# A stack of graph layers in lots: layer 3's first message three lots sooner, and a new plan of who makes which blocks

## The reference, cut to what matters

```python
h = relu(layernorm(x));  x = x + L0(h)      # pairwise attention
h = relu(layernorm(x));  x = x + L1(h)      # edge-gated aggregation
h = relu(layernorm(x));  x = x + L2(h)      # masked attention with tanh and exp
h = relu(layernorm(x));  x = x + L3(h)      # 5 steps of a gated recurrent unit
# L0: for all pairs of nodes i, j of a batch
pre = s1[i] + s2[j] + b                     # 256 features
e[i, j] = sum(a * leaky_relu(pre)) + adj    # then softmax over j, times x, sigmoid
# L3: one step
m = adj @ h;  z, r = gates(m, h);  hv = tanh(... m, r * h);  h = (1 - z) * h + z * hv
```

## Time and profile before

| | us |
|---|---|
| median of 3 runs | 5592.85 |
| lowest and highest | 5590.37, 5593.27 |
| the profiled execution, its own time | 5579.68 |
| its span, first to last instruction | 5577.9 |

### The profile page before, as it was taken

The page is one execution under the profiler, slowest core; times in us unless marked ns, Lnnn a source line. Parts: engine busy times, 40 slices in busy tenths (PEclk is TensorE's granted clock), DMA queues, the critical chain, the costliest instruction groups (busy, mean ns, idle before and its releaser), DMA issues.

```text
span 5577.9 us, 115796 instructions
## 1 busy us (share of the span) xinstructions
PE 5428.9 (97%) x38790; PEld 2133.7 (38%) x38790; DVE 5093.6 (91%) x9843; ACT 5086.3 (91%) x13332; POOL 4831.1 (87%) x9606
## 2 busy tenths in 40 slices
PE   8999999999999999999999999999999999999997
PEld 2333333333333333333333433333333333333334
DVE  8999999999998999999999999999999999999993
ACT  8999999999999999999999999999999999999993
POOL 8988888889888888889888888888898888889880
PEclk9999999999999999999999999999999999999998
DMA  0000000000000000000000000000000000000000
GB/s 14 3 4 7 7 6 3 6 7 7 6 7 3 6 7 7 6 3 6 7 7 6 5 4 7 7 7 6 3 6 7 7 6 3 6 7 7 6 6 6
DMA packets 44233, 33.97 MB, mean 6 GB/s; under 512 B 4736, under 2 KB 39552, under 8 KB 43648
## 3 DMA queue, kind: packets, MB, share of 16 engines
q1 hardware_dynamic: 43648, 26.56, 1.6%
HBM read 9.77 MB, written 8.39 MB: 3 GB/s over the span
## 4 chain that ended last, share of the span: by engine, by line
PE 93%; POOL 2%; DVE 2%; issue 2%; ACT 1%; DMA 0%; SPq 0%; POOLq 0%; DVEq 0%
PE S L1108 58%; PE R L1052 15%; PE S L1052 5%; PE W L1052 4%; PE V L1052 3%; PE R L1250 3%; POOL ring L570 2%; PE R L1258 1%; PE S L1099 1%; ACT ring L902 1%; PE V L1135 1%; DVE ring L699 1%; POOL signed L561 1%; PE R L1147 1%; PE W L1147 0%
## 5 line engine op out<-in xcount | busy, mean ns | idle before, releaser
L902 ACT ACTIVATE ring<-V,U_minus 128x256 f32<-128x256 f32 x10496 | 4114.8, 645 | 5.6 <-issue 5.6
L1108 PE MATMUL S<-ring,a_window 128*32 128x512 f32 x30720 | 3493.8, 598 | 107.9 <-issue 79.6
L570 POOL TENSOR_SCALAR ring<-W,U 128x256 f32<-128x256 f32 x7040 | 3424.6, 501 | 19.6 <-PE S L1108 19.6
L699 DVE TENSOR_TENSOR ring<-U,W 128x1024 f32<-128x1024 f32 (+2 forms) x2592 | 2662.7, 1064 | 7.1 <-ACT V L926 7.1
L1108 PEld LDWEIGHTS S<-ring,a_window 128*32 128x32 f32 x30720 | 914.4, 110 | 2396.8 <-issue 2349.2
L561 POOL TENSOR_SCALAR signed<-W_signed,U_ceiling,U_floor 128x256 f32<-128x256 f32 x2048 | 1166.5, 571 | 105.2 <-DVE ring L690 104.9
L694 DVE TENSOR_TENSOR ring<-U,W 128x256 f32<-128x256 f32 x2176 | 854.5, 409 | 0.1
L690 DVE SCALAR_TENSOR_TENSOR ring<-W,U,signed 128x256 f32<-128x256 f32 x2048 | 825.0, 470 | 2.2 <-POOL signed L561 2.2
L532 POOL TENSOR_TENSOR rstd<-var,minus_half 128x4 f32<-128x4 f32 (+1 forms) x160 | 148.8, 930 | 309.6 <-DVE var L725 171.6
L1052 PE MATMUL R<-mT,W 128*128 128x512 f32 (+1 forms) x640 | 334.0, 604 | 2.7 <-ACT mT L1012 2.7
L1052 PE MATMUL R<-AT,h 128*128 128x256 f32 x1264 | 326.9, 404 | 2.1 <-ACT h L1024 2.1
(11 more groups left out here) (185 smaller groups left out, 4282.7 us busy)
## 6 DMA issues: line engine op xcount, KB each, us to landing
X<-in_x SPq DMA_DIRECT2D x64, 128.0 KB, 2.1
X_held<-X SPq DMA_DIRECT2D x32, 256.0 KB, 2.4
out<-OUT SPq DMA_DIRECT2D x64, 128.0 KB, 1.9
edge<-in_L_gnn_w_w SPq DMA_DIRECT2D x3, 128.0 KB, 2.1
A<-in_adj SPq DMA_DIRECT2D x1, 256.0 KB, 2.7
Wn<-in_L_gnn_Wn SPq DMA_DIRECT2D x1, 128.0 KB, 2.5
Wm<-in_L_gnn_Wm SPq DMA_DIRECT2D x1, 128.0 KB, 2.5
weight<-in_L_gnn_u_w SPq DMA_DIRECT2D x2, 64.0 KB, 2.1
```

Source lines behind the costliest of these rows:

```text
L570: last = gp.tensor_scalar(ring[:, place, g, half * N:(half + 1) * N], W[:, y, c], LARGEST, U[:, y, c, i:i + 1], ALU.min, ALU.max)
L699: piece = dve.tensor_tensor(ring[:, place, g:g + groups].rearrange("p g (h j) -> p g h j", h=NB), u.unsqueeze(3).to_broadcast([P, groups, ...
L902: last = act.activation(ring[:, place, g, half * N:(half + 1) * N], W_scalar[y][:, c * N:(c + 1) * N], ACT.Relu, bias=U_minus[:, y, c, i:i ...
L1108: last = pe.matmul(S[y][g * ROWS:(g + 1) * ROWS, :], a_window[:, c, ROWS - 1 - row:2 * ROWS - 1 - row], ring[:, place, g], start=False, st ...
```

## The change

The transposes of layer 3 and its h3T copy move to lots 115 and 118, and the first message, alone of all steps, to lot 115, so that TensorE does both behind lot 112. The output copy moves from lot 113 to 112. The plan books half of each stage's cost 3 lots ahead of the stage (`AHEAD`), has other numbers for several stages, one more entry for GpSimd (7 at each half's start) and a lower start cost for GpSimd's share.

```diff
-LN3 = dict(stats=107, factors=109, norm=111, transpose=118, copy=120)
-L3_FROM, L3_PERIOD = 118, 25
-L3 = dict(message=0, ..., transpose=21, back=23)
+LN3 = dict(stats=107, factors=109, norm=111, transpose=115, copy=118)
+L3_FROM, L3_PERIOD, L3_FIRST_MESSAGE = 118, 25, 115
+L3 = dict(message=0, ..., transpose=21, out=22, back=23)

-... POOL_BLOCK, POOL_START, VECTOR_SUMMED, POOL_SIGNED = ... 4.5, 1.0, 3.92, 5.33
+... POOL_BLOCK, POOL_START, VECTOR_SUMMED, POOL_SIGNED = ... 4.5, 0.1, 3.92, 5.3
+AHEAD = 3

+    def book(costs, t, cost):
+        costs[t % LOTS] += cost / 2
+        costs[(t - AHEAD) % LOTS] += cost / 2
     def put(costs, table, at, **stages):
         for name, cost in stages.items():
-            costs[at + table[name]] += cost
+            book(costs, at + table[name], cost)

-        put(scalar, POST[h], half, exp=10, copy=4.8, tanh=5)
+        put(scalar, POST[h], half, exp=8, copy=3, tanh=5)
-        put(scalar, PRE[h], half, norm=7.7, copy=3.6, evacuate=30)
+        put(scalar, PRE[h], half, norm=7.7, copy=2.7, evacuate=32)
+        book(pool, half, 7)
-        put(scalar, ln, 0, norm=10, copy=4.8)
+        put(scalar, ln, 0, norm=15.4, copy=4.8)
-        for stage, cost in dict(update=6, state=18).items():
+        for stage, cost in dict(update=7, state=18, out=6 if s == STEPS - 1 else 0).items():

         def layer3_at(turn, t):
-            pair = turn.m - 1 if t >= L3_FROM else turn.m - 2
-            step, p = divmod((t - L3_FROM) % LOTS, L3_PERIOD)
+            pair = turn.m - 1 if t >= L3_FIRST_MESSAGE else turn.m - 2
+            if t == L3_FIRST_MESSAGE:
+                step, p = 0, L3["message"]
+            else:
+                step, p = divmod((t - L3_FROM) % LOTS, L3_PERIOD)
+                if step == 0 and p == L3["message"]:
+                    step = STEPS

-                    if p == L3["back"] and s == STEPS - 1:
+                    if p == L3["out"] and s == STEPS - 1:
```

More of the change, by code:

```diff
@@ L100 @@
 L2 = dict(project=78, copy=81, scores=86, tanh=89, exp=90, mask=93, aggregate=103, residual=106)
-LN3 = dict(stats=107, factors=109, norm=111, transpose=118, copy=120)
-L3_FROM, L3_PERIOD = 118, 25
-L3 = dict(message=0, copy=3, gates=5, reset=9, update=11, candidate=13, z_gate=15, tanh=16, state=19, transpose=21, back=23)
+LN3 = dict(stats=107, factors=109, norm=111, transpose=115, copy=118)
+L3_FROM, L3_PERIOD, L3_FIRST_MESSAGE = 118, 25, 115
+L3 = dict(message=0, copy=3, gates=5, reset=9, update=11, candidate=13, z_gate=15, tanh=16, state=19, transpose=21, out=22, back=23)
 def layer3_lot(s, stage):
@@ L116 @@
 DVE_REST_TURNED, DVE_REST_ALL = 6, 7
-VECTOR_BLOCK, VECTOR_START, SCALAR_BLOCK, POOL_BLOCK, POOL_START, VECTOR_SUMMED, POOL_SIGNED = 2.67, 0.69, 3.57, 4.5, 1.0, 3.92, 5.33
+VECTOR_BLOCK, VECTOR_START, SCALAR_BLOCK, POOL_BLOCK, POOL_START, VECTOR_SUMMED, POOL_SIGNED = 2.67, 0.69, 3.57, 4.5, 0.1, 3.92, 5.3
+AHEAD = 3
 LARGEST = 3.4028234e38
@@ L147, in stage_costs @@
     for s in range(STEPS):
-        for stage, cost in dict(update=6, state=18).items():
-            vector[layer3_lot(s, stage)] += cost
+        for stage, cost in dict(update=7, state=18, out=6 if s == STEPS - 1 else 0).items():
+            book(vector, layer3_lot(s, stage), cost)
         for stage, cost in dict(copy=4.8, reset=5.7, z_gate=5.7, tanh=5.7, back=4.8 if s < STEPS - 1 else 0).items():
-            scalar[layer3_lot(s, stage)] += cost
+            book(scalar, layer3_lot(s, stage), cost)
     return vector, scalar, pool
```

## The result

| | before | after |
|---|---|---|
| median | 5593.27 us (5 runs, 5590.37 to 5596.44) | 5534.1 us (5 runs, 5529.25 to 5551.77) |
| profiled execution | 5579.68 us | 5551.77 us |
| ratio | | 0.9899 [0.9884, 0.9915] |

The change saves 1.0% (59 us); 5533 was predicted. The two profiled executions differ by 28 us only: that of before is the fastest of its kernel here, that of after the slowest of its five.

What follows compares the result with a forecast made beforehand. Bound: TensorE's work, one stall per turn and lost clock. 30 turns x 2.25 us (0.85 stall, 1.4 clock) = 67.5, less 7.7 for turns 0 and 1, is 60 us: 5592.85 to 5533 us; range 5474 to 5577.

Steps and rivals of the forecast that it cites:

- Ceiling: Most that could be gained: stall before lot 115 plus lost clock, 4.0 us a turn, 121 us over 30 turns.
- x, the shift's lateness: GpSimd's layer-3 shift after lots 98 to 109 comes 0.8 us later, for two more blocks of 0.47 us.
- upper bound of 1.9: Largest lateness in us of GpSimd's layer-3 shift, with both added blocks at the longest seen, 1.02 us each.
- Stall left: From lot 115 to the first gate matmul, 1.75 of 2.62 us remain in pieces; 0.85 us a turn gained.
- the walk: Turn 14 followed through lots 115 to 120 and mT: small waits remain, 0.85 us gained; chance 0.45.
- predicted near 50: TensorE's waits in turns 2 to 30 of the changed kernel: near 50 us instead of 76.
- under 0.7 named as the sign: Sign in the trace: several waits under 0.7 us before lots 115 to 120 replace the 2.45 us wait.
- The clock: Half-clock stretches behind the wait before lot 115 vanish, as small waits keep full clock: 1.4 us a turn.
- the rival in which the clock stays: Half-clock stretches remain despite smaller waits or have another cause: only 18 us gained, 5575 us; chance 0.13.
- Turns 0 and 1: GpSimd's extra blocks at the start cost 7.7 us: 5.8 in turn 0, 1.9 in turn 1.
- The tail: The final 134 us, without ring lots and in the same order, change by nothing.
- Lot 83: Thinnest place elsewhere in the turn: ScalarE's blocks there keep 0.4 us to spare, so nothing new waits.

Runs made afterwards that it cites:

- message alone: Changed kernel's stage order with the block shares of the kernel before: 5513.77 us, ratio 0.9845; on a third chip ratio 1.0053.
- plan alone: Kernel before with only the changed kernel's block shares, all stages where they were: 5612.23 us, ratio 1.0021.
- filled wait: Kernel before with five extra matmuls, their result overwritten, ahead of lot 115's wait: 5556.61 us, ratio 0.9919.
- relieved plan: Changed kernel's stage order, shares of the kernel before except in nine lots (fewer GpSimd blocks before, fewer ScalarE blocks after layer 3's norm): 5497.62 us, ratio 0.9844.
- early shift: Changed kernel with lots 104 to 106 at (3,1,4), three GpSimd blocks fewer: 5677.26 us, ratio 1.0153; on a third chip 5487.83 us profiled, others 5649.04 to 5674.62.
- the first four experiments: Kernel before unchanged, moved stages with old shares, new shares with old stages, and five extra matmuls in the wait: 5594.9, 5513.77, 5612.23, 5556.61 us.
- the second profile of before: Kernel before, unedited, run and profiled again: median 5594.9 us of 11 runs, ratio 0.9993; profiled execution 5602.8 us.
- The second profile of after: Changed kernel, unedited, run again on a third chip: profiled execution 5548.77 us, the five others 5638.6 to 5654.24 us.

## Why the prediction was right, and which of its steps were not

The forecast of 5533 us met 5534.1, and the mechanism is shown: message and transposes fill the wait (message alone keeps the gain, plan alone has none), and the half clock hangs on the idling (filled wait). Turn by turn, the terms that made up the sum were off in both directions, and part of the agreement is their compensation.

- **Ceiling.** Turn 14 without its stall was put at 169.6 - 2.62 = 167.0 us. The relieved plan, 167.9 us with a wait of 0.73, bears it out (167.2 without it), and early shift at 168.0 lies above it.
- **x, the shift's lateness: 0.8 predicted, 1.6 measured in turn 14.** This is the step that was off most: two blocks at 0.47 us. Between the two profiles of turn 14 the two more blocks cost 1.36 us, since four of the 24 ring blocks are long ones of 0.9 us and more, where three of 22 were. On the chip of the first four experiments the same two blocks cost 0.8 us (18.5 to 19.3), near the prediction: what differs is the kernel before, whose turn 14 in the first profile is of the shorter kind. It stays inside the upper bound of 1.9. The rest of x is the wait before, which ends 0.22 us later as seen from lot 98, in place of the 0.1 us sooner of the prediction.
- **Stall left: 1.75 of 2.62 us predicted, about 2.7 measured** (169.7 - 167.0); the stretch from lot 113 to lot 121, 12.3 us where 9.8 would do, holds 2.5 of it. With x = 1.6 the walk's own working gives 1.75 + 0.8 = 2.55. So against turn 14 nothing of the stall is gained, where 0.85 us a turn was forecast; against the 170.2 us of a full-clock turn in the second profile of before it is 0.5 us. It only came in pieces: 45.7 us of waits, predicted near 50, and matmuls that run slower inside their groups. The lots named as ScalarE's (117 to 120, then mT) do wait for it: in turn 14 its last block of each ends 0.1 us before the lot's first matmul. But the largest piece is before lot 115, 0.8 us in half of the turns and 1.2 in the others, where 0.2 was walked out and under 0.7 named as the sign; that too is the later shift.
- **The clock: 1.4 us a turn predicted, 1.6 measured** by the filled wait. No half clock is left in turns 2 to 30 of after, where no wait is over 1.2 us: the rival in which the clock stays fell. The rule of the page "TensorE: Matmul & The Clock Gate" of the Trainium skill (Why this matters for your kernels), weighed in the prediction, stands against this, and the filled wait decides it: only the idling of some 2.5 us a turn was taken away, and the half clock went.
- **Turns 0 and 1: 7.7 us predicted, 2.6 measured** in the profiles, +4.9 in turn 0 (5.8 predicted) and -2.3 in turn 1 (160.0 to 157.7). The sum's 30 turns are turns 1 to 30, since turn 31 has no such wait, so for turn 1 it booked 1.9 - 2.25, and for both turns together 5.4 us, against the 2.6. Part of what turn 1 gained beyond this is that its waits of 2.3 and 2.4 us before lots 46 and 94, and the half clock with them (0.97 for the turn), are gone: its longest wait is 1.2 us and its clock 1.00.
- **The tail: nothing predicted, 6.8 us measured** in the profile of after (133.7 to 140.5). Its instructions are the same; the clock of the stretch is 0.83 for 0.87. The change doesn't make it: early shift has a tail of 140.6 us at 0.83 in one profile and of 127.6 at 0.94 in the other. Over the fourteen profiles the tail is 127 to 141 us long, mostly the shorter the higher its clock. The second profile of after had the long one too (140.8).
- **Lot 83** had 0.40 us left, 0.4 predicted. No new wait, as forecast.

In sums: the windows of the profiles give 39 us from turns 2 to 30, less 2.6, less 0.7 in turn 31 and less 7.4: the 28 measured (the window of turns 2 to 30 of after ends 0.9 us too early, as that of the tail begins; the two cancel in the sum). Medians give 59. The difference is the choice of executions: that of before is 13.6 us below its median, that of after 17.7 above. A tail of 127 in place of 140.5 us would account for 13 of the 17.7; that is an estimate from the other kernels' tails, since the shorter executions of after have no trace. That the prediction's 60 us came out is then partly luck: x was taken too short by 0.8 us a turn against turn 14, and the other profile of before is 0.8 us a turn longer than the one that was read (171.8 for 171.0, 0.6 of it at full clock). The two cancel.

**What stays open.** Which of the two conditions of GpSimd an execution gets. All five timed executions that the 1.0% rests on lie within 23 us of each other, and the profiled one is tight (472 ns). On the third chip the same kernel ran at 5639 to 5654 us five times of six, 0.9 to 1.1% slower than the kernel before: so the gain of 1.0% holds for the condition in which it was measured, and not for each chip. There is no trace of these five, so that they are spread ones is inferred from their times. The kernel before stayed between 5572 and 5608 us on every chip, one outlier left out, whatever the others did beside it. The relieved plan kept its gain in the spread condition. Whether the kernel before ever ran spread is not known: both its profiles are tight (473 and 476 ns). Fewer GpSimd blocks in a row around VectorE's SBUF instructions may be what spares the relieved plan, but that is not shown, and message alone, with the same shares as the kernel before, lost 1.8% from one chip to the other. No run separates shares and stages here. A kernel that was made to give GpSimd a pause ahead of each such VectorE instruction was not tried.

## What to carry to other kernels

Where one engine waits a short time at a fixed place, look for work that is already due and can be moved into the wait; the clock that comes back can be worth more than the wait, and with this plan it was most of the steady gain or all of it. Price a block that goes to a gapless engine by a range: two cost 0.8 us in one pair of profiles here and 1.36 in another, three 1.67, where their undisturbed durations give 0.93 and 1.4. Read more than one turn and more than one execution before a term rests on the difference of two turns. And look at what GpSimd does at the places where VectorE works on SBUF operands alone in a chain that TensorE waits for: in some executions its gapless rows held such instructions for several us.

## What the hardware did that was not expected

**A VectorE instruction can be held through many GpSimd instructions.** In the spread condition `diff` took up to 4.0 us instead of 0.67, through some eight GpSimd blocks, and `half_inv` 13.6 instead of 0.165, through 29 GpSimd instructions. Neither hold ended with a pause of GpSimd. VectorE's ring blocks, with W in PSUM, kept 0.41 us. The Trainium skill, "SBUF — State Buffer" (Who interferes with whom), says that a VectorE instruction with two SBUF inputs contends with a GpSimd instruction that reads SBUF, and that who issues first keeps the shared ports for the whole instruction. The prediction had used only the one side of this, VectorE in front of GpSimd. In the tight condition the trace agrees: the median `diff` of after, 0.854 us, is its own 0.67 and less than one block of 0.47. In the spread condition it does not: the hold lasts over many GpSimd instructions. And `half_inv` has one SBUF input only, of which that sentence doesn't speak; why it was held no run here shows. Nor does every instruction with two such inputs suffer: in early shift, `rh`, `diff` and the residual `X` account for 87 of the 88 holds, while `gated` and `h3T` never take over 1 us.

**The two conditions.** The median ring block of GpSimd takes 471 to 476 ns in eight of the fourteen profiles and 487 to 492 ns in the other six. It can be read from any profile, and with the same kernel it can go with 4% of the time (early shift, 5488 and 5709 us).

**Half clock behind 2.4 us of idling.** It came in 20 of 29 turns in both profiles of before, and in none of after, where the waits are up to 1.2 us. It cost 1.6 us a turn on average, nearly two thirds of the wait that brought it.
